# A recurrent cell inside a fused network: one weight set for both digits of h, and the negated reciprocal made on VectorE

## The chip, the cores and the metric

The kernel runs on one core of one Trainium2 chip. The metric is the device time of one execution in microseconds (us), taken as the median of several runs. Five engines work at once, each through its own queue in order: PE (TensorE, with its weight loads listed apart as PEld), DVE (VectorE), ACT (ScalarE), POOL (GpSimd) and SP (SyncE, which here only starts DMAs). They wait for each other through semaphores.

## The reference

A small network on an image of 4 x 64 channels x 56 x 56, in float32. The reference works in four parts, each added to its input: an involution (7 x 7 kernels made from the pixel itself), a layer of 16 experts of which two are chosen per pixel, a 3 x 3 convolution composed of low-rank factors, and last a recurrent cell. The change is in the cell:

```python
def step(carry, xs):
    h, c = carry
    xi_t, xf_t, xg_t, xo_t = xs
    i_t = jax.nn.sigmoid(xi_t + h @ V_i)
    g_t = jnp.tanh(xg_t + h @ V_c)
    o_t = jax.nn.sigmoid(xo_t + h @ V_o)
    c_new = h * c + i_t * g_t
    h_new = o_t * jnp.tanh(c_new)
    return ((h_new, c_new), h_new)
_, hs = lax.scan(step, (h0, c0), (xi, xf, xg, xo))   # T = 3136 pixels
```

(The gate f is not used by c_new.) The scan goes over all 56 x 56 = 3136 pixels, one after the other, with 4 images and 64 channels side by side. Step n + 1 needs h of step n, so its length in time is paid 3136 times.

## The kernel before, in words

**Layout.** Two images share the 128 partitions (64 channels each). A row of the picture is 56 pixels of 2 x 2 images. All four parts of the network run in a pipeline over rows: while the cell works through row j - 6, the other parts work on rows close to j. Six head rows (`dve_head_row`, `pe_head_row` and so on) fill the pipeline with no cell in them; then a hardware loop of 50 rows runs everything, and one of 6 rows runs all but the involution. So the cell takes 56 rows of 56 steps.

**Order.** It is written by hand. Each row has 56 places `t`, one for each step of the cell. On every engine the program does the cell's step first and then the piece of other work that the table `main_places()` gives to that place: on PE `pe_fill`, on ACT `act_fill`, on DVE `dve_fill`. POOL has no step of the cell. It takes its part of the other work in a fixed sequence (`pool_row`): 50 rows have seven rounds of multiplying taps (L518, `PA`), multiplying the experts' hidden values (L525, `HD`) and adding up twice (L410 and L414 in `accumulate`), and one round with the product in two halves (L532).

**A step of the cell**, with the lines of the profile:

- ACT L695: tanh of the gates in PSUM to `G6` (three gates; o is taken as a tanh, so that 1 + tanh is twice the sigmoid). L698: `1 + O_MAX * G6` to four places of `O5`, 1 + o for both digits.
- DVE L909: a scan makes the new cell value `CELL` (PSUM). It needs only L695.
- ACT L701: tanh of the cell to `TC5` (PSUM), two copies.
- DVE L914: reciprocal of 1 + o, from `O5` to `O5`. It waits for L698 (`o1_done`).
- DVE L917 and L921: two scans of five elements per image. The first gives `HR`, whose element 2 is the leading digit of h in float16; the second gives `H5`, whose element 4 is what that digit leaves over. The second needs the reciprocal (`rec_done`), the first doesn't read it.
- DVE L924 and L926: h to `HIST`, and the product for the next cell value.
- PE L1273: three 128 x 128 matmuls on 4 columns for each digit, one for each gate, added to what already lies in PSUM. The first digit waits for `hd1_done`, the second for `hd2_done`. The next step's L695 waits for the last of the six (`gates_done`).

The rounding of h to a digit is done by adding the constant GRID and taking it off again inside the scan: element 1 is (1 + o) * t + GRID, element 2 multiplies that by a constant and adds another. In the kernel before, these are -1 and GRID, so element 2 is minus the digit:

```python
link(dve, dve.memset(O5[:, :, :, 2:3], -1.0))       # L946
dve.memset(TC5[:, :, 1:3], GRID).then_inc(set_dve, 2)   # L1039
```

Hence `HR` holds minus the digit, and the first three matmuls use `VN`, a negated copy of the weights `VW`, made by ACT in a head row (L737, `RECNEG_AT`). The second digit uses `VW`. The loop on PE is

```python
for done, wt, digit in ((hd1_done, VN, HR[:, :, 2]), (hd2_done, VW, H5[:, :, 4])):
    pe.wait_ge(done, 1 + n)
    for g in range(3):
        last = pe.matmul(gates[c][:, w, :, SLOT[g]], wt[:, g]..., digit, start=False, ...)
```

and each `matmul` is a weight load and a matmul in PE's queue, the wait being on the load. After the scan L909 DVE's sequencer computes the registers that later waits need (`fill_registers`), before the reciprocal.

Of the kernel before, what the change touches and what calls it, by code (L numbers as in the profile page):

```python
# [6 lines left out]
F16 = mybir.dt.float16  # L7
# [80 lines left out]
SEL_AT, WMHI_AT, W3S_AT, RECHI_AT, RECNEG_AT = (29, 30), (29, 30), 31, 33, 52  # L88
# [4 lines left out]
def build_program(nc, x, conv1_w, bn_gamma, bn_beta, bn_mean, bn_var, conv2_w, conv2_b, gate_w, gate_b,  # L93
                  w1, w2, w3, S1s, S2s, U1s, U2s, conv_bias, U_i, V_i, b_i, U_c, V_c, b_c, U_o, V_o, b_o, out):
    with ExitStack() as ctx:
# [97 lines left out]
        VN = sb("VN", [128, 3, 2, C], F16)  # L193
# [3 lines left out]
        O5 = sb("O5", [128, 2, B, 5])  # L197
        HR = sb("HR", [128, B, 5], F16)
# [50 lines left out]
        def sems(names):  # L249
# [26 lines left out]
        (dupx_done, x4_done, pre0_done, pre1_done, gates_done, step_in, o1_done, cell_done,  # L276
         t_done, rec_done, hd1_done, hd2_done, h_done, ocopy_done, oadd_done, ostored) = lstm_sems = sems(
            "dupx_done x4_done pre0_done pre1_done gates_done step_in o1_done cell_done "
            "t_done rec_done hd1_done hd2_done h_done ocopy_done oadd_done ostored")
# [409 lines left out]
        def act_row(act, j, involution, lstm, experts, pre):  # L689
            for t in range(W):  # L690
                if lstm:
                    n = (j - LAG) * W + t
                    c, w = divmod(t, HALF)
                    act.wait_ge(gates_done, 1 + n + 1)
                    act.activation(G6[:, :, 2:5], gates[c][:, w, :, :], ACT.Tanh, scale=1 / GSCALE).then_inc(step_in, 1)  # L695

                    act.wait_ge(step_in, 1 + 2 * n + 2)
                    act.activation(O5[:, :, :, 1:5:3], G6[:, :, 3:4].unsqueeze(1).broadcast_to([128, 2, B, 2]), ACT.Copy, scale=O_MAX, bias=1.0)\  # L698
                        .then_inc(o1_done, 1)
                    act.wait_ge(cell_done, 1 + n + 1)  # L700
                    act.activation(TC5[:, :, 0:4:3], CELL[:, :, 2:3].broadcast_to([128, B, 2]), ACT.Tanh, scale=0.5)\  # L701
                        .then_inc(t_done, 1)
                act_fill(act, j, t, involution, lstm, experts, pre)

        def act_head_row(act, j):

            for t in range(W):
# [27 lines left out]
                if j == 3 and t == RECNEG_AT:  # L735
                    act.wait_ge(rec_lo, 6)
                    act.activation(VN[:, :, :, :], VW[:, :, :, :], ACT.Copy, scale=-1.0).then_inc(rec_set, 1)  # L737

# [165 lines left out]
        def dve_row(dve, j, involution, lstm, experts, pre):  # L904
            for t in range(W):
                if lstm:
# [4 lines left out]
                        .then_inc(cell_done, 1)  # L911
                    fill_registers(dve, j, t, involution, lstm, experts)
                    dve.wait_ge(o1_done, 1 + n + 1)
                    dve.reciprocal(O5[:, 1, :, 3], O5[:, 1, :, 1]).then_inc(rec_done, 1)  # L914

# [21 lines left out]
        def dve_head_row(dve, j):  # L937


            for t in range(W):  # L940
                dve_fill(dve, j, t, True, False, j >= E_SKIP, j >= C_SKIP)
                if j == 0:
                    if t == CONST_AT:
                        for tile_, v in ((HIST, 0.0), (G6, 0.0), (O5, 0.0), (HR, 0.0), (H5, 0.0), (BX, 0.0), (ONEH, 1.0), (WC, 0.0)):
                            link(dve, dve.memset(tile_[:], v))
                        link(dve, dve.memset(O5[:, :, :, 2:3], -1.0))  # L946
# [38 lines left out]
        def _(dve):  # L985
# [53 lines left out]
            dve.memset(TC5[:, :, 1:3], GRID).then_inc(set_dve, 2)  # L1039
# [224 lines left out]

        def pe_row(pe, j, involution, lstm, experts, pre):
            for t in range(W):
                if lstm:
                    n = (j - LAG) * W + t
                    c, w = divmod(t, HALF)
                    for done, wt, digit in ((hd1_done, VN, HR[:, :, 2]), (hd2_done, VW, H5[:, :, 4])):  # L1270
                        pe.wait_ge(done, 1 + n)
                        for g in range(3):
                            last = pe.matmul(gates[c][:, w, :, SLOT[g]], wt[:, g].rearrange("z m c -> z (m c)"), digit,  # L1273
                                             start=False, stop=True, skip_group_check=True)
                    last.then_inc(gates_done, 1)
# [14 lines left out]
        def pe_head_row(pe, j):  # L1290
# [7 lines left out]
            if j == C_SKIP:  # L1298
                pe.wait_ge(rec_set, 2)
# [67 lines left out]
```

## Time and profile before

| | |
|---|---|
| median of 3 runs | 4139.54 us (4135.8 to 4139.91) |
| the profiled execution, its own time | 4140.52 us |
| its span (first to last instruction) | 4138.0 us |
| PE busy | 3648.5 us, 88% |
| PE weight loads | 2433.3 us, 59% |
| DVE busy | 3447.4 us, 83% |
| ACT busy | 2635.7 us, 64% |
| POOL busy | 2154.7 us, 52% |
| granted TensorE clock | 0.522 of full speed on average, half in every slice but the first two |

The cell's first step begins 199.3 us into the span, its last ends with the span. A timeline row reads: start in us, time taken in us, engine, line of the source, operation, what it writes `<-` what it reads, shapes, how many in a row (x3), and in brackets how long the engine was idle before it and what ended that. A row of merged instructions (x3) gives the first start and the time to the last end. A busy engine is no bound in itself here: the views below follow one step.

### The profile page before, as it was taken

How to read it: one execution, taken by the hardware profiler on the slowest of the kernel's cores; microseconds unless marked ns; L12 is line 12 of the kernel's file. 1: busy time of each engine (PE TensorE's matmuls, PEld its weight loads, DVE VectorE, ACT ScalarE, POOL GpSimd, SP SyncE). 2: the span in 40 equal slices, each digit the busy share in tenths (PEclk: the TensorE clock that was granted, in tenths of full speed). 3: DMA queues.
4: the chain of work that ended last, by engine and by line, in shares of the span. 5: the costliest groups of instructions: out<-in, count | busy, mean ns of one | idle time of the engine just before them, and what ended most of it. 6: DMA issues, size and time to landing. Idle time of an engine off the chain costs nothing.

```text
span 4138.0 us, 134678 instructions
## 1 busy us (share of the span) xinstructions
PE 3648.5 (88%) x35548; PEld 2433.3 (59%) x35548; DVE 3447.4 (83%) x21828; ACT 2635.7 (64%) x11666; POOL 2154.7 (52%) x3173
## 2 busy tenths in 40 slices
PE   6798888989898989898989889898989898988887
PEld 5655656555565556565656565655556565655555
DVE  6788888888888888888888888888888888887777
ACT  3366666666666666666666666666666666666565
POOL 6555555555555545555555555555555554552222
PEclk9855555555555555555555555555555555555555
DMA  5000000000000000000000000000000000000000
GB/s 72 2 1 1 1 1 1 1 1 1 1 1 1 1 1 1 1 1 1 1 1 1 1 1 1 1 1 1 1 1 1 1 1 1 1 2 1 1 1 1
DMA packets 44537, 11.06 MB, mean 3 GB/s; under 512 B 39913, under 2 KB 44010, under 8 KB 44490
## 3 DMA queue, kind: packets, MB, share of 16 engines
q1 hardware_dynamic: 42378, 10.05, 1.7%
q10 hardware_dynamic: 2112, 0.46, 0.1%
q8 instruction: 20, 0.33, 0.0%
q14 instruction: 27, 0.22, 0.0%
HBM read 7.29 MB, written 3.21 MB: 3 GB/s over the span
## 4 chain that ended last, share of the span: by engine, by line
PE 56%; ACT 18%; DVE 18%; issue 7%; POOL 1%; DMA 0%; ACTq 0%; DVEq 0%; POOLq 0%
PE GATES L1273 23%; ACT O L698 10%; ACT G L695 8%; DVE HR L917 8%; PE YB L1087 8%; DVE O L914 8%; PE YB L1238 5%; PE DB L1206 5%; PE TAPB L1074 5%; PE DB L1068 3%; PE H1B L1114 1%; PE H2B L1114 1%; PE TAPB L1121 1%; PE TAPB L1247 1%; PE GATES L1057 1%
## 5 line engine op out<-in xcount | busy, mean ns | idle before, releaser
L695 ACT ACTIVATE G<-GATES 128x12 f32<-128x12 f32 x3136 | 573.1, 183 | 1260.0 <-PE GATES L1273 1199.9
L1273 PEld LDWEIGHTS GATES<-HR,VN 128*128 128x128 f16 x9408 | 499.9, 109 | 1309.4 <-DVE HR L917 1257.9
L1273 PE MATMUL GATES<-HR,VN 128*128 128x4 f16 x9408 | 761.8, 175 | 394.6 <-DVE HR L917 263.9
L909 DVE TENSOR_TENSOR_SCAN CT<-G,CT 128x12 f32<-128x12 f32 x3136 | 588.0, 188 | 311.0 <-ACT G L695 267.4
L698 ACT ACTIVATE O<-G 128x16 f32<-128x16 f32 x3136 | 690.5, 220 | 99.0 <-ACT G L695 0.2
L914 DVE RECIPROCAL O<-O 128x4 f32<-128x4 f32 x3136 | 569.3, 182 | 197.6 <-ACT O L698 1.0
L1273 PE MATMUL GATES<-H,VW 128*128 128x4 f16 x9408 | 714.8, 170 | 0.0
L917 DVE TENSOR_TENSOR_SCAN HR<-O,CT 128x20 f16<-128x20 f32 x3136 | 612.9, 195 | 5.0
L926 DVE SCALAR_TENSOR_TENSOR CT<-HIST,CT 128x4 f32<-128x4 f32 x3136 | 523.2, 167 | 108.9
L1087 PE MATMUL YB<-HD,W 128*64 128x112 f32 x3840 | 595.1, 411 | 2.1 <-DVE HD L818 2.1
L525 POOL TENSOR_TENSOR HD<-VV,DBS 128x448 f32<-128x448 f32 x392 | 443.4, 1131 | 273.5 <-ACT DBS L687 273.5
L518 POOL TENSOR_TENSOR PA<-PA,XN 128x336 f32<-128x336 f32 x350 | 293.6, 839 | 534.1 <-ACT PA L654 534.1
L921 DVE TENSOR_TENSOR_SCAN H<-O,CT 128x20 f16<-128x20 f32 x3136 | 533.2, 170 | 0.0
L701 ACT ACTIVATE CT<-CT 128x8 f32<-128x8 f32 x3136 | 508.0, 162 | 13.5
L1273 PEld LDWEIGHTS GATES<-H,VW 128*128 128x128 f16 x9408 | 495.9, 106 | 0.0
L1074 PE MATMUL TAPB<-RED,WT 128*128 128x112 f16 x2636 | 443.6, 288 | 2.2 <-DVE PD L804 2.0
L1081 PE MATMUL H2B<-XS,WM 128*128 128x224 f16 x1920 | 427.3, 376 | 0.3 <-DVE VV L793 0.2
L1081 PE MATMUL H1B<-XS,WM 128*128 128x224 f16 x1920 | 425.3, 375 | 0.0
L924 DVE TENSOR_TENSOR HIST<-O,CT 128x4 f32<-128x4 f32 x3136 | 418.6, 133 | 0.0
L414 POOL TENSOR_TENSOR ACC<-ACC,PD 128x448 f32<-128x448 f32 x336 | 380.4, 1132 | 36.0 <-DVE PD L804 9.3
L410 POOL TENSOR_TENSOR ACC<-ACC,PA 128x336 f32<-128x336 f32 x392 | 351.4, 896 | 48.8 <-DVE ACC L804 36.0
L1238 PE MATMUL YB<-N,WC 128*128 (+1 forms) x1044 | 371.4, 459 | 0.0
(238 smaller groups left out, 5589.9 us busy)
## 6 DMA issues: line engine op xcount, KB each, us to landing
out_dram<-OUT SPq DMA_DIRECT2D x112, 28.0 KB, 2.0
X<-in_x_dram SPq DMA_DIRECT2D x4, 672.0 KB, 13.1
STG<-in_L_ffn_w_dram SPq DMA_DIRECT2D x4, 512.0 KB, 12.5
U<-in_L_conv_U2s_dram SPq DMA_DIRECT2D x1, 972.0 KB
W<-in_L_ffn_w_dram SPq DMA_DIRECT2D x1, 512.0 KB, 11.3
X<-in_x_dram ACTq DMA_DIRECT2D x4, 112.0 KB, 3.1
S<-in_L_conv_S1s_dram SPq DMA_DIRECT2D x1, 108.0 KB
S<-in_L_conv_S2s_dram SPq DMA_DIRECT2D x1, 108.0 KB
```

Source lines behind the costliest of these rows:

```text
L695: act.activation(G6[:, :, 2:5], gates[c][:, w, :, :], ACT.Tanh, scale=1 / GSCALE).then_inc(step_in, 1)
L698: act.activation(O5[:, :, :, 1:5:3], G6[:, :, 3:4].unsqueeze(1).broadcast_to([128, 2, B, 2]), ACT.Copy, scale=O_MAX, bias=1.0)\
L909: dve.tensor_tensor_scan(CELL.rearrange("z b k -> z (b k)"), G6[:, :, :].rearrange("z b k -> z (b k)")[:, 0::2], ADD3.rearrange("z b k -> ...
L914: dve.reciprocal(O5[:, 1, :, 3], O5[:, 1, :, 1]).then_inc(rec_done, 1)
L917: dve.tensor_tensor_scan(HR[:, :, :].rearrange("z b k -> z (b k)"), O5[:, 0].rearrange("z b k -> z (b k)"), TC5.rearrange("z b k -> z (b k ...
L921: dve.tensor_tensor_scan(H5[:, :, :].rearrange("z b k -> z (b k)"), O5[:, 1].rearrange("z b k -> z (b k)"), TC5.rearrange("z b k -> z (b k ...
L926: dve.scalar_tensor_tensor(out=ADD3[:, :, 2], in0=HIST[:, t, :], scalar=0.5, in1=CELL[:, :, 2], op0=ALU.mult, op1=ALU.mult).then_inc(step_ ...
L1074: last = pe.matmul(bank[:, m * TOK:(m + 1) * TOK], WT[:, i * K7 + j0 + m].rearrange("z p g c -> z (p g c)"), RED[:, :], start=(m == 0), st ...
L1081: last = pe.matmul(bank[:, m * 2 * TOK:(m + 1) * 2 * TOK], WM[:, which, part, EG * k + m, :], XS[:, :], start=(m == 0 and part == 0), stop ...
L1087: last = pe.matmul(YE[64 * p:64 * p + 64, :], W3[:, EG * k + m, :], HD[:, k % 2, m, p, :], start=first, stop=(k == NG - 1 and m == EG - 1) ...
L1238: last = pe.matmul(YC, WC[:, k, :], N3[:, j + (N3_TOP - 5 + di), :, dj:dj + W], start=(k == 0), stop=(k == 8), skip_group_check=True)
L1273: last = pe.matmul(gates[c][:, w, :, SLOT[g]], wt[:, g].rearrange("z m c -> z (m c)"), digit, start=False, stop=True, skip_group_check=True)
```

## The change

It has two parts.

**PE.** `VN` is gone: both digits use `VW`. For each step the first weights are loaded by an instruction of their own ahead of the wait for the first digit, and the matmul behind that wait loads nothing. The first digit takes the gates in the order 0, 1, 2; the second begins with gate 2, whose weights are still in the array, so its first matmul loads nothing either, and goes on with 1 and 0. Six loads a step become four loads behind a wait or a matmul, and one ahead of the first wait.

**Signs and the reciprocal.** The constants of the scan become +1 and -GRID, so `HR` holds the digit itself. The second scan then needs minus the reciprocal of 1 + o. DVE makes -(1 + o) itself from `G6` by a `tensor_scalar` into a new tile `NEG` (128 x 4, in SBUF) right behind L909, and takes the reciprocal of `NEG` behind a wait on `neg_done`. The semaphore `o1_done` is gone; ACT's L698 stays, since both scans read 1 + o.

```diff
+        NEG = sb("NEG", [128, B])
-        VN = sb("VN", [128, 3, 2, C], F16)
...
-                    act.activation(O5[:, :, :, 1:5:3], G6[:, :, 3:4]..., ACT.Copy, scale=O_MAX, bias=1.0)\
-                        .then_inc(o1_done, 1)
+                    act.activation(O5[:, :, :, 1:5:3], G6[:, :, 3:4]..., ACT.Copy, scale=O_MAX, bias=1.0)
...
-                if j == 3 and t == RECNEG_AT:
-                    act.wait_ge(rec_lo, 6)
-                    act.activation(VN[:, :, :, :], VW[:, :, :, :], ACT.Copy, scale=-1.0).then_inc(rec_set, 1)
...
+                    dve.tensor_scalar(NEG[:, :], G6[:, :, 3], -O_MAX, -1.0, ALU.mult, ALU.add).then_inc(neg_done, 1)
                     fill_registers(dve, j, t, involution, lstm, experts)
-                    dve.wait_ge(o1_done, 1 + n + 1)
-                    dve.reciprocal(O5[:, 1, :, 3], O5[:, 1, :, 1]).then_inc(rec_done, 1)
+                    dve.wait_ge(neg_done, 1 + n + 1)
+                    dve.reciprocal(O5[:, 1, :, 3], NEG[:, :]).then_inc(rec_done, 1)
...
-                        link(dve, dve.memset(O5[:, :, :, 2:3], -1.0))
+                        link(dve, dve.memset(O5[:, :, :, 2:3], 1.0))
...
-            dve.memset(TC5[:, :, 1:3], GRID).then_inc(set_dve, 2)
+            link(dve, dve.memset(TC5[:, :, 1:2], GRID))
+            dve.memset(TC5[:, :, 2:3], -GRID).then_inc(set_dve, 2)
...
+        def multiply_loaded(pe, out, weights, moving):
+            return pe.add_instruction(mybir.InstMatmult(
+                name=nc.get_next_instruction_name(), engine=mybir.EngineType.PE, start_tensor_calc=False, stop_tensor_calc=True,
+                ldweights=False, tile_size=(128, 128), tile_position=(0, 0), bass_skip_group_check=True,
+                ins=[pe.lower_ap(moving), pe.lower_ap(weights)], outs=[pe.lower_ap(out)]))
...
-                    for done, wt, digit in ((hd1_done, VN, HR[:, :, 2]), (hd2_done, VW, H5[:, :, 4])):
-                        pe.wait_ge(done, 1 + n)
-                        for g in range(3):
-                            last = pe.matmul(gates[c][:, w, :, SLOT[g]], wt[:, g].rearrange("z m c -> z (m c)"), digit,
-                                             start=False, stop=True, skip_group_check=True)
+                    weights = [VW[:, g].rearrange("z m c -> z (m c)") for g in range(3)]
+                    pe.ldweights(weights[0], tile_position=(0, 0))
+                    pe.wait_ge(hd1_done, 1 + n)
+                    multiply_loaded(pe, gates[c][:, w, :, SLOT[0]], weights[0], HR[:, :, 2])
+                    for g in (1, 2):
+                        pe.matmul(gates[c][:, w, :, SLOT[g]], weights[g], HR[:, :, 2], start=False, stop=True, skip_group_check=True)
+                    pe.wait_ge(hd2_done, 1 + n)
+                    multiply_loaded(pe, gates[c][:, w, :, SLOT[2]], weights[2], H5[:, :, 4])
+                    for g in (1, 0):
+                        last = pe.matmul(gates[c][:, w, :, SLOT[g]], weights[g], H5[:, :, 4], start=False, stop=True,
+                                         skip_group_check=True)
                     last.then_inc(gates_done, 1)
```

PE's queue at place 1 of a row, before (a matmul stands here for its load and itself; the wait is on the load):

```order
L1114 MATMUL H1B<-SL,MEAN 128x224 [waits sq_done,slot1_done,xn4_done,xs_done]
L1271 REGISTER_ALU
L1273 MATMUL GATES<-HR,VN 128x4 [waits hd1_done]
L1273 MATMUL GATES<-HR,VN 128x4 x2
L1273 MATMUL GATES<-H,VW 128x4 [waits hd2_done]
L1273 MATMUL GATES<-H,VW 128x4 x2
```

The same place in the changed kernel:

```order
L1114 MATMUL H1B<-SL,MEAN 128x224 [waits sq_done,slot1_done,xn4_done,xs_done]
L1280 LDWEIGHTS VW
L1281 REGISTER_ALU
L1267 MATMUL GATES<-HR,VW 128x4 [waits hd1_done]
L1284 MATMUL GATES<-HR,VW 128x4 x2
L1267 MATMUL GATES<-H,VW 128x4 [waits hd2_done]
L1288 MATMUL GATES<-H,VW 128x4 x2
```

The load of the first gate's weights now stands ahead of the wait for the first digit; both waits stand on matmuls that load nothing (L1267).

DVE's queue in a step with no other work, before:

```order
L909 SCALAR_TENSOR_TENSOR CT<-G,CT 128x12 [waits step_in]
L890 ISA
L914 RECIPROCAL O<-O 128x4 [waits o1_done]
L917 SCALAR_TENSOR_TENSOR HR<-O,CT 128x20 [waits t_done]
L921 SCALAR_TENSOR_TENSOR H<-O,CT 128x20 [waits rec_done]
```

and in the changed kernel:

```order
L905 SCALAR_TENSOR_TENSOR CT<-G,CT 128x12 [waits step_in]
L909 TENSOR_SCALAR NEG<-G 128x4
L886 ISA
L912 RECIPROCAL O<-NEG 128x4 [waits neg_done]
L916 SCALAR_TENSOR_TENSOR HR<-O,CT 128x20 [waits t_done]
L920 SCALAR_TENSOR_TENSOR H<-O,CT 128x20 [waits rec_done]
```

A DVE instruction has come in between the first scan and the reciprocal, both of its tiles are in SBUF, and the reciprocal now waits for it in place of ACT. (ISA is the register work of `fill_registers`.) POOL's queue is unchanged.

## Rows read from the trace of the kernel before

**Rows 1.** Timeline of one step, all engines: start us, us, instruction.
```profile
2001.28 0.18 ACT L695 ACTIVATE G<-GATES 128x12 f32<-128x12 f32 x1 [0.20 <-PE GATES L1273]
2001.49 0.22 ACT L698 ACTIVATE O<-G 128x16 f32<-128x16 f32 x1
2001.50 0.19 DVE L909 TENSOR_TENSOR_SCAN CT<-G,CT 128x12 f32<-128x12 f32 x1
...
2001.72 0.16 ACT L701 ACTIVATE CT<-CT 128x8 f32<-128x8 f32 x1
2001.75 0.18 DVE L914 RECIPROCAL O<-O 128x4 f32<-128x4 f32 x1
...
2001.91 0.20 DVE L917 TENSOR_TENSOR_SCAN HR<-O,CT 128x20 f16<-128x20 f32 x1
2002.02 0.17 DVE L921 TENSOR_TENSOR_SCAN H<-O,CT 128x20 f16<-128x20 f32 x1
2002.11 0.13 DVE L924 TENSOR_TENSOR HIST<-O,CT 128x4 f32<-128x4 f32 x1
2002.16 0.15 PEld L1273 LDWEIGHTS GATES<-HR,VN 128*128 128x128 f16 x3 [0.39 <-DVE HR L917]
...
2002.24 0.16 PEld L1273 LDWEIGHTS GATES<-H,VW 128*128 128x128 f16 x3
2002.26 0.23 PE L1273 MATMUL GATES<-H,VW 128*128 128x4 f16 x3
...
2002.33 0.50 PEld L1081 LDWEIGHTS H2B<-XS,WM 128*128 128x128 f16 x4
...
2002.53 0.18 ACT L695 ACTIVATE G<-GATES 128x12 f32<-128x12 f32 x1 [0.65 <-PE GATES L1273]
```

**Rows 2.** Timeline, POOL and DVE, head rows: a copy and a cast beside POOL.
```profile
45.67 1.13 POOL L414 TENSOR_TENSOR ACC<-ACC,PD 128x448 f32<-128x448 f32 x1
...
46.14 0.73 DVE L843 COPY SL<-RES 128x112 f32<-128x112 f32 x1
46.88 0.65 POOL L419 TENSOR_TENSOR ACC<-ACC 128x224 f32<-128x224 f32 x1
46.94 0.62 DVE L854 CAST IXF<-IX 112x4 f32<-112x4 uint32 x1
```

**Rows 3.** The same engines in a row of the main loop: two tensor_scalars of one size.
```profile
2033.68 1.64 POOL L378 TENSOR_TENSOR RS_Y<-VE,CST 112x8 f32<-112x8 f32 x1 [7.81 <-ACT VE L618]
2033.76 0.29 DVE L860 TENSOR_SCALAR DM<-IOT,IXF,PW 112x16 f32<-112x16 f32 x1
...
2035.40 1.18 POOL L381 TENSOR_TENSOR RSE<-RS_Y,CST 112x256 f32<-112x256 f32 x2
...
2036.29 0.33 DVE L860 TENSOR_SCALAR DM<-IOT,IXF,PW 112x16 f32<-112x16 f32 x1
```

**Rows 4.** The source lines L914 and L854: ns least/median/most, first and last start.
```profile
L914 DVE RECIPROCAL O<-O x3136: 180/182/184, 199.8 to 4133.1; 128x4 f32<-128x4 f32 x196
L854 DVE CAST IXF<-IX x62: 156/163/616, 18.9 to 4068.7; 112x4 f32<-112x4 uint32 x62
```

**Rows 5.** Timeline of one of POOL's rounds, main loop (POOL alone).
```profile
2057.73 0.84 POOL L518 TENSOR_TENSOR PA<-PA,XN 128x336 f32<-128x336 f32 x1 [1.84 <-ACT PA L654]
2058.87 1.13 POOL L525 TENSOR_TENSOR HD<-VV,DBS 128x448 f32<-128x448 f32 x1 [0.30 <-ACT DBS L687]
2059.96 0.90 POOL L410 TENSOR_TENSOR ACC<-ACC,PA 128x336 f32<-128x336 f32 x1
2060.94 1.13 POOL L414 TENSOR_TENSOR ACC<-ACC,PD 128x448 f32<-128x448 f32 x1
```

**Rows 6.** Timeline of ACT over the same stretch: where steps begin.
```profile
2056.49 0.18 ACT L695 ACTIVATE G<-GATES 128x12 f32<-128x12 f32 x1 [0.52 <-PE GATES L1273]
...
2057.75 0.18 ACT L695 ACTIVATE G<-GATES 128x12 f32<-128x12 f32 x1 [0.21 <-PE GATES L1273]
...
2059.00 0.18 ACT L695 ACTIVATE G<-GATES 128x12 f32<-128x12 f32 x1 [0.20 <-PE GATES L1273]
```

More of the change, by code:

```diff
@@ L87 @@
 COMPOSE_AT = ({19: 4, 24: 4, 29: 4, 34: 4, 39: 4, 44: 4}, {14: 4, 19: 4, 24: 4, 29: 4, 34: 4, 39: 1})
-SEL_AT, WMHI_AT, W3S_AT, RECHI_AT, RECNEG_AT = (29, 30), (29, 30), 31, 33, 52
+SEL_AT, WMHI_AT, W3S_AT, RECHI_AT = (29, 30), (29, 30), 31, 33
 CONST_AT, IDUP_AT, SELZ_AT = 30, 35, 40
@@ L273, in build_program @@
             "conv_done slot3_done slot2_done res4a_done res4_done")
[L276 to L279, printed above, removed]
+        (dupx_done, x4_done, pre0_done, pre1_done, gates_done, step_in, cell_done,
+         t_done, neg_done, rec_done, hd1_done, hd2_done, h_done, ocopy_done, oadd_done, ostored) = lstm_sems = sems(
+            "dupx_done x4_done pre0_done pre1_done gates_done step_in cell_done "
+            "t_done neg_done rec_done hd1_done hd2_done h_done ocopy_done oadd_done ostored")
         counted = norm_sems + inv_sems + gate_sems + expert_sems + row_sems + lstm_sems
@@ L697, in act_row @@
                     act.wait_ge(step_in, 1 + 2 * n + 2)
-                    act.activation(O5[:, :, :, 1:5:3], G6[:, :, 3:4].unsqueeze(1).broadcast_to([128, 2, B, 2]), ACT.Copy, scale=O_MAX, bias=1.0)\
-                        .then_inc(o1_done, 1)
+                    act.activation(O5[:, :, :, 1:5:3], G6[:, :, 3:4].unsqueeze(1).broadcast_to([128, 2, B, 2]), ACT.Copy, scale=O_MAX, bias=1.0)
                     act.wait_ge(cell_done, 1 + n + 1)
@@ L1298, in pe_head_row @@
             if j == C_SKIP:
-                pe.wait_ge(rec_set, 2)
+                pe.wait_ge(rec_set, 1)
+                pe.wait_ge(rec_lo, 6)
             for t in range(W):
```

## The prediction, written before the changed kernel ran

> **What bounds the kernel.** I read the page's chain of waits first (most of it is the cell's own line on PE and its lines on ACT and DVE), then the timeline of one step. The reader is to see in it that a step is one chain from tanh to tanh of the gates, and where each link waits [rows 1]. Call the start of L695 T = 2001.28. The cell's scan starts at T + 0.22, ACT's tanh of it at T + 0.44, the scan for HR at T + 0.63 (0.03 behind that tanh's end), the scan for H at T + 0.74. HR's first weight load starts at T + 0.88, 0.05 behind HR's end; the load for H's digit at T + 0.96, 0.05 behind H's end (2002.19); the next tanh comes at T + 1.25. The page counts 3136 such steps, and 3136 x 1.25 = 3920 of the span's 4138 us; the cell-free head is the rest. PE sat idle 0.39 before that first load, and DVE's reciprocal (T + 0.47) isn't in the chain: it starts 0.03 later than ACT's tanh and ends when HR's scan starts. What lengthens H's scan or what leads to it lengthens all 3136 steps.
>
> **The loads on PE.** In the old order H's digit is three loads and three matmuls: the loads start at 2002.24, the next line's first load at 2002.33, so one pair takes 0.03; the first matmul starts 0.02 behind its load [rows 1]. HR's three pairs take 0.08 and end just as H arrives, so what the change saves in HR's digit (the load ahead of the wait) only lets PE wait for H sooner: nothing. In H's digit the first matmul can start with the semaphore, at 2002.24; two pairs of 0.03 follow, and the last matmul starts at 2002.30 and not at 2002.32. That is 0.02 per step. Bounds: nothing, if a matmul behind a wait costs what its load did; two pairs, 0.06, if H were no bound. I take 0.02, since H's arrival and the first load coincide in the row: 3136 x 0.02 = 63 us to gain. The Trainium skill ("TensorE: Matmul & The Clock Gate", what happens when you issue a matmul) says that PE pulls weight loads ahead of matmuls in flight; here the old load started only with its semaphore [rows 1], so by that rule too a load behind a wait isn't hidden, and one ahead of it is.
>
> **The small ones.** ACT's L698 stays, and it still ends (T + 0.43) where the tanh begins, so the semaphore taken off it frees nothing. The copy VN leaves one head row and one more constant is set there: under 1 us, both in the head. DVE's other work follows L926 and is shifted with it; the new instruction stands in DVE's idle time between T + 0.41 and T + 0.47 and in the scan's shadow. No DMA is added or moved.
>
> **The new instruction if nothing holds it.** The trace has no such instruction. Two scans in a row start 0.11 apart, and the 128 x 4 product for HIST takes 0.13 [rows 1]: so NEG starts at T + 0.33, ends at T + 0.46, and the reciprocal can start 0.03 later, at T + 0.49 and not T + 0.47. Its 0.18 and 0.03 put H at T + 0.70 at the earliest; H starts at T + 0.74 anyway. Free, then, with 0.04 to spare. The dearer bound: the scan's whole 0.19 and the 0.29 of the tensor_scalar with two pointer scalars [rows 3], with which H starts at T + 0.94, 0.20 late in each step, +627 us. The nearest row is the one of the same size, so I take "free".
>
> **What holds it.** NEG is a tensor_scalar from SBUF to SBUF, and POOL is busy 52% of the span. Rows of the head show what a DVE instruction of that sort does when POOL is in the middle of one: the copy issued at 46.14 ends at 46.87, 0.07 behind POOL's L414 (46.80); the cast of 4 elements issued at 46.94 takes 0.62 and ends at 47.56, 0.03 behind POOL's L419 (47.53) [rows 2]. The cast's median is 0.163 [rows 4]. They wait for the end of POOL's instruction, whatever its length. A tensor_scalar of 16 elements takes 0.33 beside POOL's second L381 (ended 2036.58), again 0.03 behind its end, and 0.29 beside L378, which doesn't hold it [rows 3]. The reciprocal, 3136 times from SBUF to SBUF with POOL busy half of the time, took 0.180 to 0.184 [rows 4]: it is never held. So the work moves to an instruction that can be held, in front of one that can't. Holding needs no great size: the cast has four elements for each partition, as NEG has.
>
> The Trainium skill ("SBUF — State Buffer", who interferes with whom) puts it as a rule: copy, cast and tensor_scalar in a two-port mode take, as an exclusive lock, the port pair that VectorE shares with GpSimd, and the second comer waits for the whole of the other's instruction. The rows of copy, cast and L860 agree with it; L378 is an exception to it.
>
> **The price.** Let POOL's instruction end E behind T and be running at T + 0.33 to 0.35. NEG ends at E + 0.03, the reciprocal starts 0.03 later and takes 0.18, H follows 0.03 behind: E + 0.27. Against 0.74, the step is longer by E - 0.47.
>
> Now one round of POOL [rows 5, 6]. Its PA starts 1.24 behind the T of its step a (2056.49), its HD 1.12 behind the T of step b (2057.75), the adding of PA 1.09 behind HD, that of PD 0.98 behind that one. With a bare step of 1.23:
> - a: nothing runs at 0.35; b begins at 1.23. PA runs from 1.24 to 2.08, ends 0.85 behind b: +0.38.
> - c begins at 2.84. HD runs from 1.23 + 1.12 = 2.35 to 3.48, ends 0.64 behind c: +0.17.
> - d begins at 4.24. The first addition (0.90) runs from 3.44 to 4.34, the second from 4.44 (its product comes late by 0.02) to 5.57, 1.33 behind d: +0.86. Then e, free.
>
> That is +1.41 per round of five steps. In a row six rounds are of this kind: 8.5 us. The same walk through POOL's other instructions gives 1.4 for the round k = 0, which follows a train of fifteen short ones, 0.4 for L381, and 0.1 for the rest: 10.4 us in a row. 56 steps x 0.02 = 1.1 come off. So +9.3 in each of 50 rows, 465 us. The six last rows have no PA and no additions: 4.9 - 1.1 = 3.8 each, 23 us. Sum against the profiled execution's 4140.5: 4140.5 + 465 + 23 = 4628.5; the median of the runs is 1 us below it, so 4628.
>
> Bounds of this term: NEG's moment of asking 0.02 earlier, 1.0 less in a row; 0.07 later, 0.9 more; the 0.47 moved by 0.05, 1.6 less or 0.8 more; no saving on PE, 0.7 more. If only half of POOL's instructions hold it (as L378 doesn't), some 240 less. If POOL's next instruction in a train comes before NEG, waits double in places: some 200 more. 4450 to 4800.
>
> **The rivals.**
> 1. NEG isn't held: its input has a stride and its scalars are constants, which no instruction of the trace combines. For it: the only tensor_scalar seen reads pointer scalars too, and these may be what waited. Against it: cast and copy have no pointer scalars and waited. Then only the 0.02 counts: 4140.5 - 63 - 1 = 4077, faster. It decides from the first step: either the new L909 takes one length throughout or it doesn't. Chance 0.12.
> 2. NEG isn't held but is slower to make than I take it: scan 0.19, NEG 0.13, so the reciprocal at T + 0.57 and H at T + 0.78, +0.04 - 0.02 = 0.02 per step: 4203. Against it: scans do overlap [rows 1]. Chance 0.03.
> 3. The loads save nothing, since a matmul without a load still takes a load's time: beside the forecast that makes 4628 + 50 x 0.7 + 6 x 1 = 4670; it lies in its range. Alone with rival 1 it would give 4139, no change: 0.01 of that rival's chance.
>
> **How the numbers follow.** The forecast, NEG held by POOL, has 0.85; rival 1 0.12, rival 2 0.03. Faster than before ends only rival 1 but for its 0.01 of no change: 0.11 faster, 0.01 same (within 0.2%, about what a measurement of this kernel can tell from none), 0.88 slower. The forecast's own range, 4450 to 4800, has nearly all of its 0.85, so it stands as the range, and rivals 1 and 2 are outside it.
>
> **What would show it.** Right: the new L909 has a least time near 0.13 and a most over 1 us; the reciprocal before HR's scan starts 0.03 behind it; steps b, c and d of a round are long and a and e short, at 1.23; POOL's instructions keep their lengths and their busy share falls; PE's idle time before the first digit grows. H's last matmul starts 0.06 and not 0.08 behind the semaphore of H. Wrong: one length of L909 beside a busy POOL, and steps of 1.23 all along (rival 1) or 1.27 (rival 2).

## The result, and the profile after

The changed kernel takes 4445.57 us (median of 4 runs, 4443.81 to 4448.19) against 4139.73 (4 runs, 4135.8 to 4140.35) for the kernel before on the same chip: 1.0741 times as long, 95% interval 1.0723 to 1.076. The forecast was 4628 with a range from 4450, so the direction was right and the time fell 4 us below the range. Of the 488 us that were forecast on top, 306 came.

The page of the profile, its head, the queue that fetches instructions, the chain of waits and two groups of instructions:

```profile
span 4442.1 us, 134735 instructions
...
PE 3724.1 (84%) x35548; PEld 2723.3 (61%) x32412; DVE 3839.8 (86%) x24965; ACT 2636.5 (59%) x11665; POOL 2160.3 (49%) x3173
...
q14 instruction: 276, 2.26, 0.2%
...
DVE 72%; PE 12%; issue 9%; ACT 5%; POOL 1%; DVEq 0%; DMA 0%; ACTq 0%; POOLq 0%
DVE NEG L909 18%; DVE O L912 12%; DVE HR L916 8%; DVE VV L789 6%; PE GATES L1267 5%; DVE PD L800 5%; DVE H L920 5%; DVE CT L925 5%; DVE CT L905 5%; ACT G L695 4%; DVE HIST L923 3%; PE GATES L1288 2%; PE DB L1068 1%; PE GATES L1284 1%; DVE XC L768 1%
...
L909 DVE TENSOR_SCALAR NEG<-G 128x4 f32<-128x4 f32 x3136 | 818.3, 261 | 3.3
...
L414 POOL TENSOR_TENSOR ACC<-ACC,PD 128x448 f32<-128x448 f32 x336 | 380.1, 1131 | 165.3 <-DVE PD L800 162.1
```

The chain, in which PE had 56% before, is now DVE for 72%, with NEG (L909) in front at 18%. Three things are to be seen beside that. NEG takes 261 ns on average. POOL's addition L414 now waits 162.1 us in all for DVE's product PD. And 276 packets of instructions are fetched where there were 27 (the experiments show that they are DVE's). The source lines of NEG and the reciprocal, to be read beside the old reciprocal in [rows 4]:

```profile
L909 DVE TENSOR_SCALAR NEG<-G x3136: 153/160/873, 196.1 to 4437.0; 128x4 f32<-128x4 f32 x196
```

```profile
L912 DVE RECIPROCAL O<-NEG x3136: 179/180/182, 196.3 to 4437.2; 128x4 f32<-128x4 f32 x196
```

A plain step, all engines, as in [rows 1]:

```profile
1740.72 0.18 ACT L695 ACTIVATE G<-GATES 128x12 f32<-128x12 f32 x1 [0.63 <-PE GATES L1288]
...
1740.94 0.19 DVE L905 TENSOR_TENSOR_SCAN CT<-G,CT 128x12 f32<-128x12 f32 x1
...
1741.03 0.16 DVE L909 TENSOR_SCALAR NEG<-G 128x4 f32<-128x4 f32 x1
1741.16 0.16 ACT L700 ACTIVATE CT<-CT 128x8 f32<-128x8 f32 x1
1741.23 0.18 DVE L912 RECIPROCAL O<-NEG 128x4 f32<-128x4 f32 x1
...
1741.35 0.20 DVE L916 TENSOR_TENSOR_SCAN HR<-O,CT 128x20 f16<-128x20 f32 x1
1741.46 0.17 DVE L920 TENSOR_TENSOR_SCAN H<-O,CT 128x20 f16<-128x20 f32 x1
1741.52 0.10 PEld L1280 LDWEIGHTS <-VW 128*128 128x128 f16 x1 [0.28 <-issue]
...
1741.60 0.17 PE L1267 MATMUL GATES<-HR,VW 128*128 128x4 f16 x1
...
1741.95 0.18 ACT L695 ACTIVATE G<-GATES 128x12 f32<-128x12 f32 x1 [0.18 <-PE GATES L1288]
```

NEG starts at T + 0.31 and ends at T + 0.47, the reciprocal starts 0.04 behind it, and both scans start at T + 0.63 and T + 0.74, as before. The step is 1.23 and no longer 1.25. This is the forecast's case in which nothing holds NEG, within 0.02.

Now one of POOL's rounds, POOL alone, as in [rows 5]:

```profile
1741.96 0.84 POOL L518 TENSOR_TENSOR PA<-PA,XN 128x336 f32<-128x336 f32 x1 [2.45 <-ACT PA L654]
1743.15 1.13 POOL L525 TENSOR_TENSOR HD<-VV,DBS 128x448 f32<-128x448 f32 x1 [0.35 <-ACT DBS L687]
1744.24 0.89 POOL L410 TENSOR_TENSOR ACC<-ACC,PA 128x336 f32<-128x336 f32 x1
1745.50 1.13 POOL L414 TENSOR_TENSOR ACC<-ACC,PD 128x448 f32<-128x448 f32 x1 [0.37 <-DVE PD L800]
```

DVE over the same stretch:

```profile
1742.26 0.57 DVE L909 TENSOR_SCALAR NEG<-G 128x4 f32<-128x4 f32 x1
...
1743.90 0.41 DVE L909 TENSOR_SCALAR NEG<-G 128x4 f32<-128x4 f32 x1
...
1744.95 0.39 DVE L800 TENSOR_TENSOR PD<-TAPB,XN 128x224 f32<-128x224 f32 x1
1745.28 0.19 DVE L905 TENSOR_TENSOR_SCAN CT<-G,CT 128x12 f32<-128x12 f32 x1
1745.38 0.16 DVE L909 TENSOR_SCALAR NEG<-G 128x4 f32<-128x4 f32 x1
```

In the step that starts at 1741.95, PA ends at 1742.80 and NEG at 1742.83. In the next, HD and L410 run into each other: HD ends at 1744.28, NEG at 1744.31. NEG is let go although POOL's next instruction has by then begun (L410 at 1744.24), so the waits don't double, as one bound of the forecast allowed. The mechanism is the one forecast, to the 0.03. The third NEG, at 1745.38, is not held, since L414 starts only at 1745.50. The forecast had L414 running through that step and charged +0.86 for it.

Averaged over 30 rows of the main loop, a row takes 75.94 and not 70.21: 5.73 more, where 9.3 was forecast.

### The profile page after: what moved, and what is told of

It is laid out like the page before. It is cut to its first block, busy times and chain, and to the rows that moved or that the text cites. A ratio compares the mean times of both kernels' runs of the same rounds, so it can differ in the third digit from the quotient of the medians.

```text
span 4442.1 us, 134735 instructions
## 1 busy us (share of the span) xinstructions
PE 3724.1 (84%) x35548; PEld 2723.3 (61%) x32412; DVE 3839.8 (86%) x24965; ACT 2636.5 (59%) x11665; POOL 2160.3 (49%) x3173
## 4 chain that ended last, share of the span: by engine, by line
DVE 72%; PE 12%; issue 9%; ACT 5%; POOL 1%; DVEq 0%; DMA 0%; ACTq 0%; POOLq 0%
DVE NEG L909 18%; DVE O L912 12%; DVE HR L916 8%; DVE VV L789 6%; PE GATES L1267 5%; DVE PD L800 5%; DVE H L920 5%; DVE CT L925 5%; DVE CT L905 5%; ACT G L695 4%; DVE HIST L923 3%; PE GATES L1288 2%; PE DB L1068 1%; PE GATES L1284 1%; DVE XC L768 1%
## 5 line engine op out<-in xcount | busy, mean ns | idle before, releaser
L1267 PE MATMUL GATES<-HR,VW 128*128 128x4 f16 x3136 | 530.1, 169 | 618.6 <-DVE HR L916 515.4
L1284 PEld LDWEIGHTS GATES<-HR,VW 128*128 128x128 f16 x6272 | 420.1, 107 | 925.1 <-issue 850.2
L909 DVE TENSOR_SCALAR NEG<-G 128x4 f32<-128x4 f32 x3136 | 818.3, 261 | 3.3
L698 ACT ACTIVATE O<-G 128x16 f32<-128x16 f32 x3136 | 690.0, 220 | 99.0 <-ACT G L695 0.2
L912 DVE RECIPROCAL O<-NEG 128x4 f32<-128x4 f32 x3136 | 565.8, 180 | 118.4 <-DVE NEG L909 11.6
L1280 PEld LDWEIGHTS <-VW 128*128 128x128 f16 x3136 | 456.4, 146 | 343.8 <-issue 309.5
L1284 PE MATMUL GATES<-HR,VW 128*128 128x4 f16 x6272 | 617.7, 169 | 0.0
L1288 PE MATMUL GATES<-H,VW 128*128 128x4 f16 x6272 | 616.1, 169 | 0.0
L916 DVE TENSOR_TENSOR_SCAN HR<-O,CT 128x20 f16<-128x20 f32 x3136 | 580.9, 185 | 0.0
L920 DVE TENSOR_TENSOR_SCAN H<-O,CT 128x20 f16<-128x20 f32 x3136 | 567.6, 181 | 0.0
L1267 PE MATMUL GATES<-H,VW 128*128 128x4 f16 x3136 | 524.4, 167 | 0.0
L414 POOL TENSOR_TENSOR ACC<-ACC,PD 128x448 f32<-128x448 f32 x336 | 380.1, 1131 | 165.3 <-DVE PD L800 162.1
L1288 PEld LDWEIGHTS GATES<-H,VW 128*128 128x128 f16 x6272 | 412.2, 105 | 20.5
```

Source lines behind the costliest of these rows:

```text
L909: dve.tensor_scalar(NEG[:, :], G6[:, :, 3], -O_MAX, -1.0, ALU.mult, ALU.add).then_inc(neg_done, 1)
L912: dve.reciprocal(O5[:, 1, :, 3], NEG[:, :]).then_inc(rec_done, 1)
L916: dve.tensor_tensor_scan(HR[:, :, :].rearrange("z b k -> z (b k)"), O5[:, 0].rearrange("z b k -> z (b k)"), TC5.rearrange("z b k -> z (b k ...
L920: dve.tensor_tensor_scan(H5[:, :, :].rearrange("z b k -> z (b k)"), O5[:, 1].rearrange("z b k -> z (b k)"), TC5.rearrange("z b k -> z (b k ...
L1267: return pe.add_instruction(mybir.InstMatmult(name=nc.get_next_instruction_name(), engine=mybir.EngineType.PE, start_tensor_calc=False, st ...
L1284: pe.matmul(gates[c][:, w, :, SLOT[g]], weights[g], HR[:, :, 2], start=False, stop=True, skip_group_check=True)
```

## The experiments

Two theories stood at the start. **Held by POOL**: nearly all of the loss is NEG waiting for POOL's instruction in progress. **Any further instruction**: the loss comes from DVE having one instruction more in each step, of whatever kind. Places are the 56 steps of a row, 0 to 55. Every run has its own runs of the kernel before beside it (medians of 4132 to 4134), so ratios are compared. Rows and steps of the kernel before are read from its one traced execution, of 4140.5; that is 6 to 8 more, 0.1 to 0.15 of a row, so differences of rows with it are no finer than that.

### NEG by an instruction with one source and no scalars

```diff
-                    dve.tensor_scalar(NEG[:, :], G6[:, :, 3], -O_MAX, -1.0, ALU.mult, ALU.add).then_inc(neg_done, 1)
+                    dve.tensor_reduce(NEG[:, :], G6[:, :, 3:6:2], AX.X, ALU.add, negate=True).then_inc(neg_done, 1)
...
+                        link(dve, dve.memset(G6[:, :, 5:6], 1.0 + 2.0 ** -23))
```

It leaves out the factor O_MAX in NEG.

> The changed kernel, with NEG made by a tensor_reduce (o plus a constant that lies beside it in G6, negated) in place of the tensor_scalar; the constant is 1 + 2^-23 and the factor O_MAX is left out of NEG alone. Same place, same tiles, same number of DVE instructions. Theory A (a tensor_scalar from SBUF to SBUF waits out POOL's instruction, and a reduction doesn't; PE saves 0.023 us a step; DVE's loop body has grown from 472 to 528 instructions and is fetched again by DMA in every row, 0.9 us a row): about 4113 us, NEG of one length throughout, q14 still with 4 to 5 packets a row. Rival B (any instruction there costs, by its place between the scan and the reciprocal): no faster than 4400.

Measured: 4127.99 against 4131.96, ratio 0.999 (0.998 to 0.9999). The source line of NEG:

```profile
L909 DVE TENSOR_REDUCE NEG<-G x3136: 146/153/165, 197.6 to 4122.3; 128x4 f32<-128x8 f32 x196
```

All 3136 take 146 to 165 ns, with POOL busy as before. Place for place against the changed kernel, a row is 5.76 shorter. 5.7 of it lies at 19 places, those where a POOL instruction meets NEG. 5.76 x 50 = 288, and the 6 last rows add 29, 317 against the 315 between the two traced spans: this is the loss, and "any further instruction" has fallen as its main cause. But it isn't all clear gain. A plain step is 1.225 (0.022 less than before, 1.2 a row) and yet a row is 70.18, only 0.03 less than before. The rows show where the 1.2 went: places 0, 27 and 40 are 0.28, 0.25 and 0.17 longer than before, places 8 and 12 0.13 and 0.10, and the rest, some 0.3, is spread over others. Places 8 and 12, some 13 us in 50 rows, are most of what the time lies above the expected 4113; the last section has their cause.

### The same tensor_scalar in the kernel before, read by nobody

```diff
                         .then_inc(cell_done, 1)
+                    dve.tensor_scalar(DUM[:, :], G6[:, :, 3], -O_MAX, -1.0, ALU.mult, ALU.add)
                     fill_registers(dve, j, t, involution, lstm, experts)
```

> The kernel before, with one more DVE instruction behind the cell's scan: the tensor_scalar of NEG, written to a tile that nothing reads; nothing waits for it by semaphore. Theory A: it is held by POOL as NEG is, and the old PE order gives 0.023 us a step back, but no semaphore lies between it and the reciprocal: 4440 to 4520 us. Rival B (the loss is the reciprocal's new wait for NEG): under 4200.

Measured: 4334.26, ratio 1.0488 (1.0471 to 1.0506): below the 4440 of the first theory and far over the 4200 of the rival. POOL and DVE in one round:

```profile
1702.85 0.84 POOL L519 TENSOR_TENSOR PA<-PA,XN 128x336 f32<-128x336 f32 x1 [2.52 <-ACT PA L655]
```

```profile
1703.17 0.55 DVE L913 TENSOR_SCALAR DUM<-G 128x4 f32<-128x4 f32 x1
1703.63 0.17 DVE L916 RECIPROCAL O<-O 128x4 f32<-128x4 f32 x1
```

The instruction is held to 0.03 behind PA's end (1703.69) although no semaphore ties anything to it: what follows on DVE stands behind it in the queue. It costs less than in the changed kernel, 2.15 a row. Where PA holds it (places 21, 26, 31, 36, 41 and 46) it is 0.13 a step less, which fits that the reciprocal doesn't wait for its result and starts 0.09 before its recorded end. But 1.29 of the 2.15 lies at places 17 and 27 alone, where POOL's instructions fall otherwise into the steps: at 17 it takes 0.19 in all, where NEG takes 0.76.

### A reciprocal in its place, read by nobody

```diff
+                    dve.reciprocal(DUM[:, :], G6[:, :, 3])
```

> The same with a reciprocal of o as the unread instruction: never held by POOL in the rows of before, and the same number of DVE instructions as the changed kernel. Theory A: only the fetching of DVE's code counts, 0.9 us in each of 50 rows: about 4185 us, with 4 to 5 packets of q14 a row and long steps at places 0, 27 and 40. Rival C (the long steps at these places in the changed kernel are POOL's doing, and fetching is hidden): 4140, the packets beside it or not.

Measured: 4169.54, ratio 1.0092 (1.0075 to 1.0109). The extra reciprocal takes 158 to 180 ns in all 3136 cases, never held, yet the kernel is 38 longer than before. A row is 0.64 longer, and places 0, 27 and 40 are 0.81 longer (0.31, 0.30, 0.20); the other 53 together are 0.17 shorter, about the difference between the executions named above, so they are no longer at all. 0.81 x 50 = 40 us is the whole cost. DVE at place 27, where the step begins at 1646.88:

```profile
1647.09 0.39 DVE L805 TENSOR_TENSOR PD<-TAPB,XN 128x224 f32<-128x224 f32 x1 [0.30 <-issue]
1647.40 0.18 DVE L910 TENSOR_TENSOR_SCAN CT<-G,CT 128x12 f32<-128x12 f32 x1
```

DVE sat idle for 0.30 with nothing to wait for ("issue"), and its product came too late for the scan. The queue that fetches instructions, here and in the kernel before:

```profile
q14 instruction: 275, 2.25, 0.2%
```

```profile
q14 instruction: 27, 0.22, 0.0%
```

2.25 MB instead of 0.22. In the main loop the kernel before has no such packet; here there are five in each row, at places 0, 14, 27, 40 or 41, and 54 or 55. Three of the five stand at the places with the stalls; those at 14 and 54 cost nothing that shows. DVE's loop of one row has 472 instructions before and 528 after (56 more, waits and registers counted in both). So a further theory arose: **the loop no longer fits where DVE keeps its instructions, and each row is fetched again.**

### The extra reciprocal in some steps only

```diff
+                    if t < 32:    # 504 instructions in the row; 44 in the other kernel: 516
+                        dve.reciprocal(DUM[:, :], G6[:, :, 3])
```

> The kernel before with the unread reciprocal in 32 of the 56 steps of a row: DVE's loop body has 504 instructions. Theory A (a loop body up to 512 instructions stays in place, a longer one is fetched anew in each row): no q14 packets in the main loop, the time of the kernel before. Rival D (the unread instruction itself costs, in proportion): 32/56 of the 38 us that 56 of them cost, +21 us.

> The same in 44 of 56 steps: 516 instructions. Theory A: 4 to 5 q14 packets a row again and long steps, +30 to +40 us, though only 12 instructions more than the one with 32. Rival D: 44/56 of 38, +30 us, but without packets.

Measured: 4136.76, ratio 1.0006 (0.9996 to 1.0015), with 504 instructions; 4206.81, ratio 1.0177 (1.016 to 1.0194), with 516. These kernels differ in DVE's program alone, so the packets are DVE's. The first has the 27 packets of the kernel before; the line of the second, and DVE of the second at place 0 (the step begins at 1628.81):

```profile
q14 instruction: 275, 2.24, 0.2%
```

```profile
1628.56 0.17 DVE L929 SCALAR_TENSOR_TENSOR CT<-HIST,CT 128x4 f32<-128x4 f32 x1
1630.12 0.19 DVE L910 TENSOR_TENSOR_SCAN CT<-G,CT 128x12 f32<-128x12 f32 x1 [1.40 <-issue]
```

Between 504 and 516 the fetching starts. 32 extra instructions a row cost nothing that can be told from zero, twelve more cost 70. The step at place 0 is 1.02 longer than with 504. The Trainium skill ("Runtime: NRT & Kernel Launch", instruction fetch mechanics) gives 512 instructions for such an engine and says that a branch to a target outside what is held stalls on a fetch. This threshold lies between the two runs. The same section calls the cost of crossing a block "mostly hidden". In these loops that is so for the packets at places 14 and 54, while those at 27 and 40 come with 0.2 to 0.3 in each row. Why 516 instructions cost more than 528 stays open: the step at place 0 is 1.02 longer in the one and 0.31 in the other.

### No NEG at all: six elements in the scan

```diff
-        O5 = sb("O5", [128, 2, B, 5])
+        O5 = sb("O5", [128, 2, B, 6])      # HR, H5 and TC5 likewise; one more element turns the sign
...
-                    dve.tensor_scalar(NEG[:, :], G6[:, :, 3], -O_MAX, -1.0, ALU.mult, ALU.add).then_inc(neg_done, 1)
-                    dve.wait_ge(neg_done, 1 + n + 1)
-                    dve.reciprocal(O5[:, 1, :, 3], NEG[:, :]).then_inc(rec_done, 1)
+                    dve.wait_ge(o1_done, 1 + n + 1)
+                    dve.reciprocal(O5[:, 1, :, 4], O5[:, 1, :, 1]).then_inc(rec_done, 1)
```

PE is as in the changed kernel; DVE's row has 472 instructions again.

> The changed PE order and one weight set, but no NEG: each scan has six elements for an image in place of five (minus the digit, then for the first digit times -1, for the second times +1), and the reciprocal is that of 1 + o behind o1_done, as before. DVE's loop body has 472 instructions. Theory A: PE's 0.023 us a step come off, about 0.01 is lost to the four more elements of each scan: about 4100 us, no q14 packets in the main loop, no held instruction. If PE's new order saves nothing: about 4170.

Measured: 4119.84, ratio 0.997 (0.9959 to 0.9982), no fetching in the loop. A plain step is 1.240, 0.015 more than the 1.225 of the kernel with the reduction, since H's scan starts 0.008 later and both scans are longer; 0.01 had been expected for that. It is 12 us faster than the kernel before, and faster than the changed one.

### PE's two halves apart

Both are made from the kernel with six elements. In the first the load ahead of the wait is gone, in the second the second digit loads all three weights:

```diff
-                    pe.ldweights(weights[0], tile_position=(0, 0))
                     pe.wait_ge(hd1_done, 1 + n)
-                    multiply_loaded(pe, gates[c][:, w, :, SLOT[0]], weights[0], HR[:, :, 3])
-                    for g in (1, 2):
+                    for g in (0, 1, 2):
```

```diff
-                    multiply_loaded(pe, gates[c][:, w, :, SLOT[2]], weights[2], H5[:, :, 5])
-                    for g in (1, 0):
+                    for g in (2, 1, 0):
```

> The six-element kernel with the load ahead of the wait undone: all three loads of the first digit stand behind hd1_done again; the third weights still stay for the second digit. Theory A (only what follows H's arrival counts, and the first digit's loads end by then): as fast as the six-element kernel, 12 us below the kernel before. If the load ahead matters: a load's time a step, 0.02 x 3136 = 60 us slower than that.

> The six-element kernel with the kept weights undone: the second digit loads all three weights again behind hd2_done, the first load of the first digit still stands ahead of its wait. Theory A: loses the 0.022 us a step, so some 65 us slower than the six-element kernel, about 50 us slower than the kernel before; tanh to tanh 1.26 us in a plain step and not 1.24.

Measured: 4148.69, ratio 1.0037 (1.0023 to 1.0051), a plain step of 1.253; 4188.7, ratio 1.0134 (1.0117 to 1.0151), a plain step of 1.267. So in a plain step the load ahead is worth 0.013 and the kept weights 0.027, each with the other in place; the first had been expected to be worth nothing. They don't add up: both together gave 0.022. The kernel with six elements and neither wasn't run. An estimate for it is 1.250 + 0.015 = 1.265; against that the kept weights alone gain some 0.01 and the load ahead alone nothing (1.267). H's first matmul and the next tanh, with both halves, without the load ahead, and without the kept weights (there the three matmuls are one row):

```profile
1622.55 0.17 PE L1267 MATMUL GATES<-H,VW 128*128 128x4 f16 x1
...
1622.81 0.18 ACT L694 ACTIVATE G<-GATES 128x12 f32<-128x12 f32 x1 [0.19 <-PE GATES L1288]
```

```profile
1631.43 0.17 PE L1267 MATMUL GATES<-H,VW 128*128 128x4 f16 x1
...
1631.68 0.18 ACT L694 ACTIVATE G<-GATES 128x12 f32<-128x12 f32 x1 [0.21 <-PE GATES L1286]
```

```profile
1645.90 0.24 PE L1287 MATMUL GATES<-H,VW 128*128 128x4 f16 x3
...
1646.18 0.18 ACT L694 ACTIVATE G<-GATES 128x12 f32<-128x12 f32 x1 [0.22 <-PE GATES L1287]
```

From H's first matmul to the next tanh it is 0.26, 0.25 and 0.28. In the second kernel H's first matmul comes later after T, 1.00 (1631.43 - 1630.43) against 0.98 (1622.55 - 1621.57). That fits a reading in which HR's three pairs of load and matmul, begun only with the semaphore, end just behind H and push its first matmul.

### NEG asks 0.16 later

```diff
+                        .then_inc(o1_done, 1)     # on L698
...
+                    dve.wait_ge(o1_done, 1 + n + 1)
                     dve.tensor_scalar(NEG[:, :], G6[:, :, 3], -O_MAX, -1.0, ALU.mult, ALU.add).then_inc(neg_done, 1)
```

This is for the step d in which the forecast failed: if L414 can hold NEG, and only starts too late, then a NEG that asks later must be held by it.

> The changed kernel with o1_done put back and NEG waiting for it, so that NEG asks at about 0.467 behind the start of a step's tanh G instead of 0.311. In the changed kernel POOL's second addition (L414) starts 0.434 to 0.437 behind the start of the step it falls in, 0.12 behind NEG's asking, and so never holds it. Theory A, the corrected walk (any POOL instruction in progress holds NEG to its end; L414 escaped by its start alone): a plain step is 0.137 longer (1.364) because reciprocal and H's scan move with NEG, and L414 now holds NEG to its end 1.12 later, so step d of each of the six rounds is about 0.97 longer than a plain one; a row near 88 and the whole near 5100. Theory B (this addition does not hold NEG whatever it meets, for instance because its operands are not where NEG's are): step d is as long as a plain one, no step over 2.0 in the six rounds' places d, and the whole near 4800.

Measured: 5054.04 us (one run) against 4132.35. Step d, POOL and DVE (the step begins at 1977.72, the next at 1980.07):

```profile
1978.16 1.13 POOL L414 TENSOR_TENSOR ACC<-ACC,PD 128x448 f32<-128x448 f32 x1 [0.37 <-DVE PD L801]
```

```profile
1978.19 1.12 DVE L911 TENSOR_SCALAR NEG<-G 128x4 f32<-128x4 f32 x1
1979.35 0.18 DVE L914 RECIPROCAL O<-NEG 128x4 f32<-128x4 f32 x1
```

L414 holds NEG for 1.12, 0.02 past its own end, and step d is 2.35 beside a plain one of 1.39: 0.95 more, 0.97 expected. The plain step itself is 0.03 over the expected. A row is 87.3, near 88 expected. So L414 holds NEG like the others, and in the changed kernel it was only its start, 0.12 behind NEG's asking, that saved the step.

### Both forms in one row

The scans of five elements with NEG by reduction are 0.015 shorter, those of six need no further instruction, and 504 instructions fit. So 32 of the 56 steps take the one and 24 the other, each with its own tiles. NEG leaves out O_MAX as above.

```diff
+        def five(t):
+            return t > 15 and t % 5 != 1
...
+                    if five(t):
+                        dve.tensor_reduce(NEG[:, :], G6[:, :, 3:6:2], AX.X, ALU.add, negate=True).then_inc(o1_done, 1)
```

> A candidate: 32 of the 56 steps (t > 15 and t % 5 != 1) take the scans of five elements with NEG made by a reduction of one source as in e1_neg_reduce, the other 24 the scans of six elements and no NEG as in e4_six_elements; DVE's row is 504 instructions. Leaves out O_MAX in NEG's factor. Theory A (a plain step is 0.015 shorter with five elements, 1.225 against 1.240, a reduction is never held, and 504 instructions need no refetch in the loop): 32 x 50 x 0.015 = 24 less than six elements throughout (4120 beside a kernel before of 4132), so 0.991 of the kernel before, 4095 to 4100, and no instruction packets in the main loop. Theory B (switching between two sets of tiles costs, or code is refetched at 504 instructions when they are other ones): 4115 or more, with instruction packets every row or longer steps at each change of form.

Measured: 4091.04 (a little under the expected), ratio 0.99 (0.9884 to 0.9917), a row of 69.35 against 69.87 with six elements throughout (0.52 less, 32 x 0.015 = 0.48 expected) and no fetching in the loop. It is the fastest kernel of the study, 41 us below the kernel before.

## Why the prediction was right in kind and wrong in size

A row of the main loop, by the comparison of steps place by place (us; the measured "others" is what is left to the sum):

| term | forecast | measured |
|---|---|---|
| PE, 56 x 0.02 | -1.1 | -1.23 |
| NEG held, step d of six rounds | +5.2 | 0 |
| NEG held, all else | +5.2 | +5.76 (0.76 of it at place 27) |
| instruction fetch, places 0, 27, 40 | none | +0.70 |
| places 8 and 12, and others | none | +0.50 |
| sum | +9.3 | +5.73 |

The 0.70 still has PE's gain in it, which the first line counts at all 56 places; without it the three places are 0.77 longer and the others 0.43. The six last rows came as forecast: 22 us for the 23.

- **The loads on PE: right in sum, by luck in part.** 0.02 a step was forecast and 0.022 came. But the step by which the load ahead of the wait saves nothing is wrong: with the kept weights it is worth 0.013 (six elements), and the kept weights alone, for which the 0.02 stood, some 0.01 by the estimate above. HR's pairs were read as ending "just as H arrives", and that is exactly where 0.01 decides. The sign named for it came: H's last matmul starts 0.11 behind H's end and not 0.13.
- **The small ones, and NEG if nothing holds it: right.** NEG unheld is 0.16, and the reciprocal starts at T + 0.51 and ends at T + 0.69, still ahead of H's scan at T + 0.74.
- **The reciprocal in the chain: not quite.** The prediction had it outside; the page of the kernel before gives its line 8% of the chain. It made no difference to the sum: starting 0.04 later, it moved neither scan.
- **What holds it: right.** POOL's instruction in progress holds the tensor_scalar and never the reciprocal or the reduction, though 1834 of the 3136 reciprocals before and 1889 of the 3136 reductions start in the middle of one. "Step longer by E - 0.47" gave +0.38 at PA's step and +0.17 at HD's; measured 0.41 and 0.17 in most rounds (0.25 for HD in the one shown, 0.21 and 0.37 in the round at places 41 and 42).
- **The failing step: the price of d, "+0.86".** The walk let L414 start 0.10 behind the end of the first addition, "late by 0.02" through its product. But L414 waits for DVE's product PD, which DVE makes at the end of step c. The walk stretched the steps, by 0.38 and 0.17, and kept POOL's two additions at their old distances behind HD, with 0.02 on top for PD. But PD moves with the steps by all of their stretching, and with it L414. The kernel before shows how PD lies to its step d:

```profile
2053.86 0.39 DVE L804 TENSOR_TENSOR PD<-TAPB,XN 128x224 f32<-128x224 f32 x1
...
2053.99 0.18 ACT L695 ACTIVATE G<-GATES 128x12 f32<-128x12 f32 x1 [0.65 <-PE GATES L1273]
...
2054.76 1.13 POOL L414 TENSOR_TENSOR ACC<-ACC,PD 128x448 f32<-128x448 f32 x1
```

  PD ends at T + 0.26 of step d, and L414 starts 0.51 behind that (0.44 in the other five rounds). In the changed kernel PD ends at 1745.34, T + 0.27, and L414 starts 0.16 behind it. So with PD moved in full the walk's L414 would start near T + 0.42, behind NEG's asking, where the walk had T + 0.20. In the kernel before, L414 hardly waited for PD (9.3 us in all); now 162.1. L414 starts at T + 0.43 to 0.44 of step d in each of the six rounds, and NEG has asked at T + 0.31. 0.86 x 6 x 50 = 258 us of the 488 stand on that. With NEG asking 0.16 later the hold in step d came in all six rounds.
- **Missing from the sum: the fetching of instructions.** Alone it is 0.81 a row at places 0, 27 and 40 (+38 us in all, the extra reciprocal), and here it also moves the cell's scan at place 27 to T + 0.55. NEG's asking then falls into L410, which starts at T + 0.59, and is held to L410's end:

```profile
1750.38 0.18 ACT L695 ACTIVATE G<-GATES 128x12 f32<-128x12 f32 x1 [0.58 <-PE GATES L1288]
1750.62 0.39 DVE L800 TENSOR_TENSOR PD<-TAPB,XN 128x224 f32<-128x224 f32 x1 [0.30 <-issue]
1750.93 0.18 DVE L905 TENSOR_TENSOR_SCAN CT<-G,CT 128x12 f32<-128x12 f32 x1
1750.97 0.90 POOL L410 TENSOR_TENSOR ACC<-ACC,PA 128x336 f32<-128x336 f32 x1
1751.02 0.87 DVE L909 TENSOR_SCALAR NEG<-G 128x4 f32<-128x4 f32 x1
```

  That one place is 1.02 longer than before, 0.76 of it by holding: 38 us of the whole.
- **The range and the signs.** The low end stood 178 below the forecast, while the bound "only half of POOL's instructions hold it" was put at 240 less, 4388, and left outside. In kind it was near to what happened: of the four in a round PA and HD hold NEG, L414 nothing, and L410 nothing but at place 27. The forecast had three of the four, with the longest hold on the one that wasn't. The two rivals on the other side fell with the first step: L909 has no one length beside a busy POOL, and the plain step is 1.23 and not 1.27. The signs that were named came: a least of 0.15 for L909, PE idle longer before the first digit, POOL's lengths unchanged, its busy share down from 52% to 49%, a and e short. Two did not: the most of L909, named as over 1 us, is 0.87, and d is short. These two tell which step of the forecast failed.

## What to carry to other kernels

Before an operation moves to VectorE behind a chain that sets the time, look whether it is of the kind that waits for GpSimd's instruction in progress (here tensor_scalar, copy and cast from SBUF to SBUF did, a reciprocal and a reduction of one source didn't), and choose the form that isn't held; here that was 310 us of difference, by the ratios, for the same four numbers per partition. When a walk stretches steps, move every producer of every instruction in it, not only the engine that is being priced. And count the instructions of a hardware loop on each engine before adding one per step; on the page only the line of the instruction queue tells of the fetching.

## What the runs showed of the hardware

- A held instruction of 4 elements can take as long as a POOL instruction of 448: NEG took 0.153 to 0.873 and, asked 0.16 later, up to 1.128. Its end lies 0.02 to 0.03 behind POOL's, also where POOL's next instruction has by then begun. Being read by nobody doesn't help: queue order alone makes the wait the chain's.
- The hold needs POOL's instruction to have started first: with L414 starting 0.12 behind the asking, NEG was unheld, and L414 kept its 1.13.
- DVE's loop: 504 instructions cost nothing, 516 cost 72 us and 528 cost 38 (against the kernel before), in stalls at the loop's start and at two places within. The timeline marks those looked at as "issue".
- NEG starts 0.10 behind the start of the scan in front of it or sooner, but at places 8 and 12 it starts 0.22 behind it, 0.03 after the scan has ended. These are the two places of the 56 where the instruction before the scan writes partitions that don't begin at 0 (L772 `RED[64:96]`, L819 `DP[32:64]`). It is so in the changed kernel, in the one with the reduction and, for the unread reciprocal, in the third experiment. At place 12 of the kernel with the reduction:

```profile
1616.09 0.26 DVE L819 TENSOR_TENSOR DP<-TAPB,DH 32x112 f16<-32x112 f32 x1
1616.34 0.19 DVE L905 TENSOR_TENSOR_SCAN CT<-G,CT 128x12 f32<-128x12 f32 x1
1616.56 0.17 DVE L909 TENSOR_REDUCE NEG<-G 128x4 f32<-128x8 f32 x1
```

  That step is 0.13 longer than its neighbours. The Trainium skill ("VectorE: DVE Perf Modes", two Vector instructions with no wait between them) has it that an instruction is held when its output starts in another group of 32 partitions than the last output into that memory; both places agree, and no run here moves the partitions to test it.
- Not tried: whether NEG in PSUM would escape the hold, and what in the tensor_scalar makes it wait where the reduction doesn't.
